# Gated cross-attention and routed experts on one core: stores as 96 and 4 rows at other times, last ranks and slots moved up, tile 2 in two passes, x of batch 1 between the halves of the first keys

## The reference

```python
def xattn(query, key):                       # per batch: (100 x 1024), (361 x 1024)
    e = softmax(query @ key.T, axis=-1)
    return e @ key
x = x + tanh(g_xattn) * xattn(layernorm(x), ctx)
h = layernorm(x)
logits = h @ W_gate + b_gate                 # 8 experts
top_idx = top_k(logits, 2)
y_all = relu(h @ W_e[e] + b_e[e])            # for each expert e, 1024 x 1024 weights
y = mean over the two chosen experts
x = x + tanh(g_ffn) * y
```

## Time and profile before

| | us |
|---|---|
| median of three runs | 343.68 |
| lowest and highest run | 340.76 and 344.42 |
| the profiled execution, its time | 344.42 |
| its span (first to last instruction) | 342.5 |
| TensorE busy in the span | 319.5 |

### The profile page before, as it was taken

How to read it: one execution, slowest core, us unless ns; L and a number is a source line. 1 busy time by engine, 2 the same in 40 slices (tenths; PEclk the granted TensorE clock), 3 DMA queues, 4 the chain that set the end, 5 groups by cost and what they waited for, 6 DMA issues and landing times.

```text
span 342.5 us, 4328 instructions
## 1 busy us (share of the span) xinstructions
PE 319.5 (93%) x1510; PEld 235.1 (69%) x1510; DVE 203.9 (60%) x434; ACT 122.9 (36%) x165; POOL 75.3 (22%) x91
## 2 busy tenths in 40 slices
PE   5699999999999999959999999999999999999970
PEld 5344565565665588738788888888888888888850
DVE  2324457676668886886694975755176575753220
ACT  2223434625534558013345535515032551431000
POOL 6000110100103320303334321530120333011120
PEclk9969999999999999999999999999999999999995
DMA  7999999999948799567999999998359989634152
GB/s 253 303 288 303 349 353 332 354 319 362 389 156 292 268 382 327 147 225 206 379 340 367 353 355 354 255 381 273 61 169 346 282 215 382 208 61 63 10 84 31
DMA packets 24711, 90.57 MB, mean 264 GB/s; under 512 B 3276, under 2 KB 3276, under 8 KB 24680
## 3 DMA queue, kind: packets, MB, share of 16 engines
q1 hardware_dynamic: 13752, 52.86, 43.6%
q0 software_dynamic: 7792, 25.47, 28.5%
q10 hardware_dynamic: 3136, 11.83, 10.4%
HBM read 73.63 MB, written 16.52 MB: 263 GB/s over the span
## 4 chain that ended last, share of the span: by engine, by line
PE 80%; DMA 10%; DVE 4%; POOL 1%; ACT 1%; issue 1%; SPq 0%; DVEq 0%
PE ps L449 49%; PE ps L357 11%; PE ps L382 11%; DMA hn_rows<-hn 4%; PE ps L432 4%; DMA wg<-in_L_ffn_W_gate 3%; DMA xg<-hn_rows,src_token 2%; PE ps L403 2%; PE ps L394 1%; PE ps L348 1%; DVE stats L738 1%; DVE x_all L789 1%; DMA x_all<-in_x 1%; PE ps L365 1%; POOL guess L1117 1%
## 5 line engine op out<-in xcount | busy, mean ns | idle before, releaser
L449 PE MATMUL ps<-wh,xh 128*128 128x512 f32 x256 | 83.0, 400 | 0.1
L449 PE MATMUL ps<-wl,xh 128*128 128x512 f32 x256 | 80.4, 393 | 0.3 <-issue 0.3
L881 DVE TENSOR_TENSOR wl<-raw,wh 128x1024 fp32r<-128x1024 f32 x64 | 75.6, 1219 | 8.4 <-ACT wh L632 8.1
L449 PE MATMUL ps<-wh,xl 128*128 128x512 f32 x256 | 80.2, 393 | 0.0
L632 ACT ACTIVATE wh<-raw 128x1024 fp32r<-128x1024 f32 x64 | 63.7, 1051 | 22.9 <-DMA raw<-in_L_ffn_W_e 20.9
L449 PEld LDWEIGHTS ps<-wl,xh 128*128 128x128 f32 x256 | 48.0, 188 | 11.4 <-DVE wl L881 0.7
L449 PEld LDWEIGHTS ps<-wh,xl 128*128 128x128 f32 x256 | 48.0, 188 | 10.7
L449 PEld LDWEIGHTS ps<-wh,xh 128*128 128x128 f32 x256 | 46.4, 188 | 9.3 <-DVE xl L885 0.5
L1065 POOL DMA_INDIRECT out_rows<-y,dst_token x15 | 29.0, 1933 | 107.1 <-DVE y L895 88.5
L635 ACT ACTIVATE xh<-ps 128x1024 fp32r<-128x1024 f32 x16 | 16.4, 1024 | 90.1 <-PE ps L432 90.1
L357 PE MATMUL ps<-kT,qT 128*100 128x361 f32 x128 | 43.4, 493 | 1.0 <-ACT qT L611 1.0
(11 more groups left out here) (124 smaller groups left out, 240.0 us busy)
## 6 DMA issues: line engine op xcount, KB each, us to landing
raw<-in_L_ffn_W_e SPq DMA_DIRECT2D x64, 512.0 KB, 9.2
kT<-in_ctx_cols SPq DMA_DIRECT2D x16, 722.0 KB, 11.3
ctx<-in_ctx ACTq DMA_DIRECT2D x8, 1024.0 KB, 11.1
bias<-in_L_ffn_b_e SPq DMA_DIRECT2D x8, 512.0 KB, 10.9
ctx<-in_ctx ACTq DMA_DIRECT2D x8, 420.0 KB, 14.5
hn_rows<-hn POOLq DMA_DIRECT2D x8, 400.0 KB, 9.5
out_rows<-x_all POOLq DMA_DIRECT2D x2, 1600.0 KB, 19.1
x_all<-in_x SPq DMA_DIRECT2D x7, 384.0 KB
```

What stands on the lines that cost most here:

```text
L449: mm = nc.tensor.matmul(into[:, n * HB:(n + 1) * HB], rows[:, k, :], weights[:, k, n * HB:(n + 1) * HB], start=(k == 0 and c == first), st ...
L881: nc.vector.tensor_tensor(wl[e % 2][:, k, :], raw[e % 2][:, k, :], wh[e % 2][:, k, :], ALU.subtract).then_inc(s_wl, 1)
```

## The change

1. **Stores as 96 and 4 rows.** Each store of 100 partitions (`hn` of a batch, a half of `x_all`) becomes two DMAs, of 96 and of 4 partitions. x was loaded so already.
2. **The two halves of `x_all` at other times and on other queues.** The first half is issued by ScalarE at the end of its iteration `s` = 6, behind `load_values(7)`. The second half is issued by SP behind the weights of expert 1 and a wait for `s_h` = 8, and the zeros stand behind it on SP. GpSimd issues neither.
3. **Last ranks and slots moved up.** In the LH pass of tile 0, `ranks(7)` goes from behind chunk 4 to behind chunk 0, `slots(6)` from 2 to 1, and `slots(7)` with `counts(1)` from chunk 1 of tile 1 to chunk 6 of this pass. VectorE splits chunk 0 of the weights of expert 1 ahead of `name_tokens(1)` and the other seven behind it.
4. **Tile 2 in two passes.** HH and HL of all chunks first (these wait for `xh` only), with `turn_tile(3)` behind chunk 5, then LH (this waits for `xl`). `s_wfree` counts in the first pass; a new semaphore `s_wh0free` counts the second pass, and ScalarE waits for it before it writes the high weights of expert 2.
5. **x of batch 1** is loaded between the two halves of the keys of batch 0.
6. **The tanh** go from in front of the loop to the end of ScalarE's iteration 0, behind `evacuate_probs(0)`.

```diff
+        def hidden(half, first, end):
+            rows = out[half * HALF_TOK:(half + 1) * HALF_TOK, :].rearrange("(b q) d -> q b d", q=Q)
+            return rows[first:end], x_all[first:end, half * HALF_B:(half + 1) * HALF_B, :]
@@ SP
-            load_keys(0)
+            load_keys(0, (0,))
             load_x(1)
+            load_keys(0, (1,))
             load_keys(1)
...
             for k in range(KD):
                 load_weights(1, k)
+            sp.wait_ge(s_h, B)
+            for first, end in X_PARTS:
+                sp.dma_start(*hidden(1, first, end)).then_inc(s_hstore[1], 16)
+            sp.wait_ge(s_const, 1)
+            for t in range(HALVES):
+                rows = out[N_TOK + t * P:N_TOK + (t + 1) * P, :].rearrange("p (a d) -> p a d", d=256)
+                sp.dma_start(rows, zero[...]...).then_inc(s_zero, 16)
             sp.wait_ge(s_hn, B)
@@ TensorE, LH pass of tile 0
-                if k == 2:
+                if k == 0:
+                    ranks(B - 1)
+                if k == 1:
                     slots(B - 2)
-                if k == 4:
-                    ranks(B - 1)
+                if k == 6:
+                    slots(B - 1)
+                    counts(1)
@@ TensorE, tile 1, first pass
-                if k == 1:
-                    slots(B - 1)
-                    counts(1)
@@ TensorE, tiles from 2 on
+                if n == 2:
+                    pe.wait_ge(s_xh, n + 1)
+                    for k in range(KD):
+                        tile(n, k, (HH, HL), None).then_inc(s_wfree, 1)
+                        if k == 5:
+                            turn_tile(n + 1)
                 pe.wait_ge(s_xl, n + 1)
...
-                    mm = tile(n, k)
+                    mm = tile(n, k, (LH,)) if n == 2 else tile(n, k)
@@ ScalarE
             def split_weights(e, k):
                 act.wait_ge(s_raw[e % 2][k], 16 * (e // 2 + 1))
+                if e == 2:
+                    act.wait_ge(s_wh0free, k + 1)
...
                 if 1 <= s and s + 1 < B:
                     act.wait_ge(s_att, s)
                     load_values(s + 1)
+                if s + 2 == B:
+                    act.wait_ge(s_h, HALF_B)
+                    for first, end in X_PARTS:
+                        act.dma_start(*hidden(0, first, end)).then_inc(s_hstore[0], 16)
@@ VectorE
+            split_weights(1, 0)
             name_tokens(1)
-            for k in range(KD):
+            for k in range(1, KD):
                 split_weights(1, k)
@@ GpSimd
             def store_normed(b):
                 pool.wait_ge(s_hn, b + 1)
-                g.dma_start(hn_rows[b * Q:(b + 1) * Q, :], hn[:, :]).then_inc(s_hnstore, 16)
+                for first, end in X_PARTS:
+                    g.dma_start(hn_rows[b * Q + first:b * Q + end, :], hn[first:end, :]).then_inc(s_hnstore, 16)
```

More of the change, by code:

```diff
@@ L227, in gated_block @@
         s_table = sem("tile_table_ready")
-        s_hstore = sem("h_stored")
+        s_hstore = [sem(f"h_stored{h}") for h in range(HALVES)]
         s_hnstore = sem("hn_stored")
@@ L233, in gated_block @@
         s_wfree = sem("w_used")
+        s_wh0free = sem("first_w_high_used")
         s_gath = [sem(f"gathered{t}") for t in range(2)]
@@ L293, in load_x, with load_keys @@
                     sp.dma_start(x_all[first:end, b, :], x[b, first:end, :]).then_inc(s_x[b - 1], 16)
-            def load_keys(b):
-                for h in range(2):
+            def load_keys(b, halves=(0, 1)):
+                for h in halves:
                     ks = slice(h * KD // 2, (h + 1) * KD // 2)
@@ L326, in _ @@
                 load_weights(1, k)
+            sp.wait_ge(s_h, B)
[4 more added lines that the diff above has]
+                rows = out[N_TOK + t * P:N_TOK + (t + 1) * P, :].rearrange("p (a d) -> p a d", d=256)
+                sp.dma_start(rows, zero[:, :].unsqueeze(1).to_broadcast([P, D // 256, 256])).then_inc(s_zero, 16)
             sp.wait_ge(s_hn, B)
-            sp.wait_ge(s_hstore, 16 * len(STORES))
+            for h in range(HALVES):
+                sp.wait_ge(s_hstore[h], 16 * len(X_PARTS))
             load_bias(0)
@@ L576, in _ @@
                         pe.wait_ge(s_wl, KD * e + k + 1)
-                    mm = tile(n, k)
+                    mm = tile(n, k, (LH,)) if n == 2 else tile(n, k)
                     if half == 1:
-                        mm.then_inc(s_wfree, 1)
+                        mm.then_inc(s_wh0free if n == 2 else s_wfree, 1)
                     if n + 1 < N_TILES:
-                        if k == 2:
+                        if k == 2 and n > 2:
                             turn_tile(n + 1)
@@ L682, in _ @@
                 evacuate_probs(s)
+                if s == 0:
+                    act.wait_ge(s_params, 64)
+                    nc.scalar.activation(tgx[:, :], gx[:, :], ACT.Tanh).then_inc(s_tanh, 1)
+                    nc.scalar.activation(tgf[:, :], gf[:, :], ACT.Tanh).then_inc(s_tanh, 1)
+                    act.wait_ge(s_tanh, 2)
+                    nc.scalar.mul(tgf_half[:, :], tgf[:, :], 1.0 / TOP_K).then_inc(s_tgf, 1)
                 if 1 <= s and s + 1 < B:
@@ L959, in _ @@
             split_tile(2)
-            dve.wait_ge(s_hstore, 16 * len(STORES))
+            for h in range(HALVES):
+                dve.wait_ge(s_hstore[h], 16 * len(X_PARTS))
             dve.wait_ge(s_hn, B)
@@ L1132, in _ @@
                 store_normed(s - 1)
[L1133 to L1139, removed]
-                        g.dma_start(rows, zero[:, :].unsqueeze(1).to_broadcast([P, D // 256, 256])).then_inc(s_zero, 16)
-            pool.wait_ge(s_hnstore, 16 * B)
+            pool.wait_ge(s_hnstore, 16 * len(X_PARTS) * B)
             pool.wait_ge(s_tokens, 2)
@@ L1150, in _ @@
             over, over_before = overs(pool, 0)
+            for h in range(HALVES):
+                pool.wait_ge(s_hstore[h], 16 * len(X_PARTS))
             gather_first_over(0, over, over_before)
             pool.wait_ge(s_zero, 32)
-            pool.wait_ge(s_hstore, 16 * len(STORES))
             add_tile(0)
```

18 lines of the change are left out of this document (6 added, 12 removed).

## The result

The changed kernel takes 345.63 us (median; 342.6 to 347.87), the kernel before, run between its runs, 343.17 us. The ratio is 1.0076, with an interval of 1.0047 to 1.0105: slower by 0.8%, by about 2.6 us, where 339.8 was forecast, with a range of 336.8 to 343.0.

A forecast was written before the change was run, and what follows sets the result against it. TensorE, busy for 319.5 of 342.5 us, was taken as the bound. Terms -1.7 + 1.0 - 3.5 = -4.2 us gave 340.2 or 339.5 by base, hence 339.8; own range 337.5 to 341.2, 8 in 10 from 336.8 to 343.0.

The forecast's parts named there:

- the term +1.0: Gather of tile 0: late by 1.9 us, 0.75 of it covered, costing +1.0 us; bounds 0 and 4.75.
- the first rival: The gather of tile 0 becomes the new wait: late by 4.2 us, costs 3.4, time 342.6; chance 0.13.
- The lateness: Gather of tile 0: 0.6 for the extra issue plus 1.4 for shared bandwidth, less 0.1 margin, is 1.9 us.
- Half of the bandwidth: Gather of tile 0: its 512 KB get half of some 370 GB/s beside the store, 1.4 us more.
- under "wrong": Signs against the forecast, among them a second stretch at the lower clock; no size given.
- The rule that the prediction weighed: Tile 0's gather: all queues share 16 DMA engines, so +1.0 holds; were queues independent, the sum would be 1.0 lower.
- The slower rival: At `turn_tile(0)`: the gather takes 15.2 us in a full queue, 8.1 late, costs 7.3, time 346.5; chance 0.07.
- The start, -1.7: x of batch 1 and tanh: `scores(2)` ends at 37.16 instead of 38.90, -1.7 us; bounds 0 and -3.0.
- The middle, -3.5: Tile 2: its gather comes sooner, the 3.17 us wait vanishes, two passes help; -3.5 us, bounds 0 and -3.9.
- What was costed at nothing: Tile 2's two passes, SP's wait for `s_h`, seven further `hn` stores and the moved tanh: no cost.
- a sign: At `turn_tile(4)`: a new wait for `xg` would show the forecast wrong; no size given.
- The base: Whole kernel: -4.2 us from the profiled 344.42 gives 340.2, from the median 343.68 gives 339.5; 339.8 lies between.

The follow-up runs named there:

- experiment 10: The changed kernel run again, unedited, beside the kernel before: 345.43 us against 342.13, ratio 1.0089.
- experiment 1: Changed kernel with the first half of `x_all` stored by SP behind the weights of expert 1: 342.38 us against 343.39, ratio 0.999.
- experiment 2: Changed kernel with the first half of `x_all` stored by SP behind the last chunk of expert 0's weights: 340.99 us against 343.39, ratio 0.9966.
- experiment 6: Kernel before with only the first half of `x_all` moved to ScalarE at the end of iteration 6: 348.51 us against 343.63, ratio 1.0113.
- Experiment 9: Changed kernel with 14 unused transposes of the identity on TensorE ahead of `turn_tile(0)`: 342.82 us against 344.11, ratio 0.994.
- experiment 4: Changed kernel with parts 5 and 6 undone (old order of x of batch 1 and tanh): 345.61 us against 343.39, ratio 1.0102.
- experiment 5: Kernel before with parts 5 and 6 alone (x of batch 1 and tanh moved): 342.51 us against 343.63, ratio 0.9967.
- experiment 7: Kernel before with parts 3 and 4 alone, run twice: 341.85 us against 343.63, ratio 0.9932; then 343.62 against 344.11, ratio 0.9977.
- experiment 8: Changed kernel with ScalarE storing two of the first half's four batches, SP the others behind expert 1's weights: 341.24 us against 344.11, ratio 0.991.
- experiment 3: Changed kernel with each `hn` store as one DMA of 100 rows again: 344.69 us against 343.39, ratio 1.0047.

## Why the prediction was wrong, step by step

**The step that failed is the gather of tile 0, the term +1.0.** It measured 5.0 in the profile of the result, beyond even its bound of 4.75, and 3.2 in the second profile of the same kernel (experiment 10). The mechanism, a gather made late by the store's bytes, was right; its size was not. The term was too small in two ways, the first rival in the second of them alone: it had 4.2 us of lateness, more than was measured, and 3.4 of cost.
- *The lateness.* It was sized at 0.6 + 1.4 - 0.1 = 1.9 and was 3.1: some 0.36 from the later issue against the lead (102.40 is 2.41 sooner than 104.81, where TensorE was 2.77 sooner) and 2.8 from the landing (10.41 against 7.6), less the margin of 0.1. Half of the bandwidth for the gather's own bytes was too mild. (The 370 GB/s in that step stand in none of the rows; the window that it names had 259 at a share of 0.87, some 298 at a full one, and with that the step would have given 1.8.) The `hn` store just ahead of it on GpSimd is slowed too: it landed 5.74 us after its issue before, its two parts after 8.57 and 10.04 now, the last of them at 111.62, 1.2 us ahead of the gather. That the gather has to wait for it is argued from this order, not shown. Experiments 1 and 2 take the bytes away and the wait goes or shrinks to 0.60; experiment 6 adds them to the kernel before and the wait comes.
- *The clock.* The sum let TensorE go on at full rate behind the wait. From `turn_tile(0)` to `turn_hidden(6)` it took 121.92 - 112.85 = 9.07 instead of 7.15, of which 0.75 had been idle; 9.07 - (7.15 - 0.75) = 2.67 us is work at the lower clock. The 0.75 did cover something, as argued: 3.09 + 2.67 - 0.75 = 5.0. Experiment 9 shows this as a cost of its own: 2.8 us less at this place with the wait as long. The prediction read a stretch at the lower clock at the start and listed a second one under "wrong", but gave it no price.

The rule that the prediction weighed, from the Trainium skill (DMA: Bandwidth & Descriptors, section "Issuing engines are not separate DMA queues"), says that DMAs of any engine run on the same 16 engines. The runs agree: a store on ScalarE's queue cost GpSimd's gather 2.8 us (10.41 against 7.6) in the changed kernel and 3.8 (11.41) in experiment 6. The half rate that the prediction drew from it gave 1.4, so that step was too mild, not the rule.

**The slower rival** named the right place and the wrong neighbours: it had the gather as deep in the queue as behind the weights of expert 1, but SP issued these from 109.74 on, 7.3 us after the gather. It decided from a lateness of 5.95 us on; the medians came out slower at about half of that. The clock, which had no price in it, and the smaller start are a part of the reason.

**The start, -1.7.** The mechanism was right: the keys of batch 2 end the lead, with the gap in `scores(2)`. That these keys "will not come sooner" was not: they landed at 33.26, 1.35 ahead of the 34.61, and so the lead in the profile is 2.9. But the size is no constant. In seven profiles with the new order `turn_hidden(0)` starts between 35.81 and 37.27, in two at 38.44 and 39.31 (mean of the nine: 37.2); in five with the old order, between 36.56 and 38.77 (mean 38.0). So the new order is worth about 0.9, and the profile of before, at 38.74, was at the late end of its five. A value nearer to the bound of 0 would have been better: experiment 4 loses nothing by the old start that its medians show, experiment 5 gains 0 to 0.7%.

**The middle, -3.5.** It measured 3.76. The store was the cause (experiment 7), and the lists came next: they were there at 140.27, but the 4-row part of the store landed still later, at 140.43, and GpSimd issued the gather at 141.03. The forecast of 136.6 for the store and 138.3 for the lists was 2 to 4 us too early; it did no harm, since TensorE too was 2.24 late by then.

**What was costed at nothing.** SP's new wait, the tanh and the extra `hn` issues show no wait on TensorE. Two passes of tile 2 neither; the 0.80 at `turn_tile(4)` was listed as a sign, not summed.

**The base.** -2.9 + 5.0 - 3.8, and 0.8 given back at `turn_tile(4)`, leave the profiled executions within some tenths of each other, as they were seen. The medians say +2.5, because the profiled before was 1.25 above its median and the profiled after 1.42 below. A part of this is the start: with the 0.9 of the means in place of the 2.9, the same sum is +1.1. The other 1.4 us stay open, since no profile shows the kernel before near its median. The stretch at the lower clock at the start is not what sets the profiled execution apart: all five profiles with the old order show it, with a mean clock of 0.69 or 0.84 from 16 to 27, and eight of the nine with the new order have 1.00 there (experiment 8 has 0.84). The windows of before, experiment 4 and the changed kernel:

```profile
16.00:27.00 11.00, 9.15 (x27) 5.13 (x28) 2.56 (x10) 3.65 (x11) 0.55 (x1) 0.69 1.03 303
16.00:27.00 11.00, 10.04 (x33) 5.35 (x34) 3.80 (x14) 3.64 (x12) 0.55 (x1) 0.84 1.03 291
16.00:27.00 11.00, 10.07 (x34) 4.88 (x32) 4.31 (x15) 3.82 (x12) 0.55 (x1) 1.00 1.03 315
```

So the new order does remove this stretch. It gains little, because TensorE then waits for the keys of batch 2, which landed between 33.3 and 36.8 with the new order and between 34.0 and 36.2 with the old.

## What to carry to other kernels

Before a transfer is moved, list what lands with no margin in the stretch it goes to, and what its bytes do there, whichever engine issues them; the same store cost some 4 us at one place and next to nothing where it was issued 19 us sooner (79.1 instead of 98.1) and its bytes filled a stretch in which the engines had been at 0.38. Price a wait of TensorE of some microseconds with the slower work behind it, not with its length alone. Where several loads bound a gain one behind the other, take the spread of their landings over several executions before the gain is put into a sum.

## What the runs showed of the hardware

- An idle wait of 3.09 us left the granted clock near 0.50 for some 6 us behind it (and 3.76 in experiment 6 likewise), but the idle 3.17 before `turn_tile(2)` in the profile of before was followed by a `turn_tile` of 1.09 us, the duration at 1.00. Within one execution, that of experiment 10, the idle 2.38 before `turn_tile(0)` was followed by slow matmuls (5.30 us for eight instead of 3.60), the idle 2.55 in `scores(2)` by matmuls at full rate (2.68 us). So the length of the wait alone does not decide, and what does is not settled here.
- The 16 KB part of the last `hn` store landed after 11.2 us, the 384 KB part, issued just ahead of it, after 6.6. The second half of `x_all` and the zeros, issued by SP from 123.87 on, moved at that time. The small part landed last and set the gather; the split is not to blame, since one store of 100 rows in its place (experiment 3) took 10.89.
- With the first half of `x_all` beside it, the gather of tile 0 landed after 12.71 and 11.41 us behind an `hn` store of 100 rows (experiments 3 and 6), and after 9.66 to 10.86 behind one of 96 and 4 rows (four profiles: the changed kernel, experiments 4, 9 and 10).
- One load of 722 KB, issued at the same place of the program, took 16.4 us in one execution of the changed kernel and 19.69 in another (experiment 10); the lead of the start hung on it.
